# Turning the row maxima of a fused attention and expert block: one square of 128 columns for four tiles of 8, and one transfer for two

## The reference

```
def xattn(query, key, value):            # 16 heads of 16, B = 4, L = 512
    q = (query @ wq.T + bq)...; k = (key @ wk.T + bk)...; v = (value @ wv.T + bv)...
    scores = einsum('bhld,bhsd->bhls', q, k) / 4
    return einsum('bhls,bhsd->bhld', softmax(scores), v)

def ffn(src):                            # self attention with rotation, then experts
    q, k = rope(src @ Wq), rope(src @ Wk_c @ Wk); v = src @ Wv_c @ Wv
    sa = softmax(q k / 4) v @ Wo
    x = rmsnorm(src + sa, n1)
    shared = swiglu(x @ W_shared_in) @ W_shared_out
    routed = sum_e swiglu(x @ W1_shared) @ W2[e] * w[:, e]     # best 2 of 4 experts of the best group
    return rmsnorm(x + shared + routed, n2)

x = x + tanh(g_xattn) * xattn(layernorm(x), ctx, ctx)
x = x + tanh(g_ffn) * ffn(layernorm(x))
```

## Time and profile before

| what | value |
|---|---|
| median of 3 runs | 798.07 us (795.81 to 799.25) |
| profiled execution | 799.23 us, span 797.5 us |
| mean granted TensorE clock | 0.983 |
| busy: TensorE, weight loads | 752.8 us (94%), 347.6 us |
| busy: VectorE, ScalarE, GpSimd | 512.8, 417.4, 225.2 us |
| turned maxima L1607 | 128 matmuls, 217 to 221 ns, from 47.9 to 525.5 us |
| copy L782 | 32, 569 to 587 ns |
| transfers of the maxima L788 | 64 issues of 4 KB |

### The profile page before, as it was taken

The page is one execution under the profiler, slowest core; times in us unless marked ns, Lnnn a source line. Parts: engine busy times, 40 slices in busy tenths (PEclk is TensorE's granted clock), DMA queues, the critical chain, the costliest instruction groups (busy, mean ns, idle before and its releaser), DMA issues.

```text
span 797.5 us, 10572 instructions
## 1 busy us (share of the span) xinstructions
PE 752.8 (94%) x3606; PEld 347.6 (44%) x3606; DVE 512.8 (64%) x776; ACT 417.4 (52%) x766; POOL 225.2 (28%) x342
## 2 busy tenths in 40 slices
PE   5889999999999999999999999999999899989994
PEld 3432343343233233233423423426645755458883
DVE  2598848847868868878797798743366022523664
ACT  3447868877758767776675777683211122222000
POOL 3451123223315405304222410010105612400654
PEclk9989999999999999999999999999999999999998
DMA  8882233226124414413411331006003824000010
GB/s 244 222 240 62 59 106 121 80 51 200 47 57 164 108 41 136 129 41 94 144 42 41 125 105 52 1 2 210 1 0 134 274 100 132 0 0 1 34 40 34
DMA packets 51316, 73.32 MB, mean 92 GB/s; under 512 B 6976, under 2 KB 42304, under 8 KB 51264
## 3 DMA queue, kind: packets, MB, share of 16 engines
q1 hardware_dynamic: 47248, 63.80, 27.0%
q0 software_dynamic: 2816, 8.46, 2.8%
q10 hardware_dynamic: 1200, 0.40, 0.2%
HBM read 45.04 MB, written 27.33 MB: 91 GB/s over the span
## 4 chain that ended last, share of the span: by engine, by line
PE 75%; DVE 13%; ACT 6%; issue 3%; DMA 1%; POOL 1%; ACTq 1%; DVEq 0%; POOLq 0%
PE ps L1479 35%; PE ps L1627 11%; PE ps L1651 11%; PE ps L1599 10%; DVE negm L1135 7%; ACT hS L891 3%; PE ps L1474 2%; DVE bst L1013 2%; PE ps L1615 1%; PE ps L1607 1%; PE ps L1538 1%; DMA bv_bc<-in_L_xattn_bv_dram 1%; ACT rows L797 1%; PE ps L1533 1%; PE ps L1559 0%
## 5 line engine op out<-in xcount | busy, mean ns | idle before, releaser
L1135 DVE TENSOR_REDUCE negm<-ps 128x2 f32<-128x1024 f32 x256 | 304.9, 1223 | 80.4 <-PE ps L1599 73.3
L891 ACT ACTIVATE hS<-ps 128x512 f32<-128x512 f32 x512 | 278.5, 600 | 106.4 <-PE ps L1651 104.5
L1651 PE MATMUL ps<-w 98*128 98x512 bf16 x512 | 168.0, 386 | 5.9 <-ACT hS L891 3.3
L1599 PE MATMUL ps<-w 96*128 96x512 bf16 x512 | 154.6, 383 | 5.5 <-DVE negm L1135 4.9
L1627 PE MATMUL ps<-hS,mix 128*17 128x512 f32 x1024 | 134.7, 598 | 0.2
L1651 PEld LDWEIGHTS ps<-w 98*128 98x128 bf16 x512 | 42.5, 97 | 153.4 <-ACT hS L891 70.6
L1599 PEld LDWEIGHTS ps<-w 96*128 96x128 bf16 x512 | 49.0, 99 | 58.6 <-DVE negm L1135 11.5
L1331 DVE SCALAR_TENSOR_TENSOR ctxs<-qk,ps 128x512 f32<-128x512 f32 x32 | 22.0, 688 | 76.6 <-ACT qk L925 76.0
L925 ACT ACTIVATE qk<-ps 128x512 f32<-128x512 f32 x32 | 19.1, 597 | 82.5 <-PE ps L1479 78.6
L1479 PE MATMUL ps<-w,hS 128*128 x256 | 57.4, 387 | 2.0 <-issue 2.0
L1479 PEld LDWEIGHTS ps<-w,hS 128*128 128x128 f32 x256 | 49.7, 195 | 9.9 <-issue 2.8
(11 more groups left out here) (209 smaller groups left out, 891.6 us busy)
## 6 DMA issues: line engine op xcount, KB each, us to landing
w<-scrq SPq DMA_DIRECT2D x32, 384.0 KB, 4.1
scrk<-mix SPq DMA_DIRECT2D x24, 256.0 KB, 2.1
scrq<-mix SPq DMA_DIRECT2D x16, 384.0 KB, 3.3
scrq<-mix SPq DMA_DIRECT2D x24, 256.0 KB, 2.5
w<-scrk SPq DMA_DIRECT2D x32, 192.0 KB, 3.0
w<-scrk SPq DMA_DIRECT2D x32, 128.0 KB, 3.0
w<-in_L_ffn_W_experts_dram SPq DMA_DIRECT2D x8, 512.0 KB, 8.0
mix<-scrf SPq DMA_DIRECT2D x4, 528.0 KB, 5.6
```

The lines of the kernel that those rows point to most:

```text
L891: nc.scalar.activation(prob[:, kt % PROB_SLOTS, s % HG, :], slot_bank(("unit", u)), ACT.Exp, scale=SC).then_inc(s_exp, 1)
L1135: V.tensor_reduce(negm[:, gi % 2, 2 * t2:2 * t2 + 2, h], ps[:, bank:bank + 2, :], AX.X, ALU.max, negate=True).then_inc(s_re, 1)
L1599: last = MM(ps[:, bank + t, :], qs[0:STK, g, h, tt * P:(tt + 1) * P], ks[0:STK, g, h, :], start=True, stop=True)
L1651: MM(take(("unit", u)), ks[:, g, h, kt * P:(kt + 1) * P], qs[:, g, h, :], start=True, stop=True).then_inc(s_sT, 1)
```

## The change

The maxima are kept with heads outside and tiles inside, `m2` becomes a full square of 128 columns per parity of the group, of which 32 hold maxima (2 parts x 4 heads x 4 tiles) and 96 are zero, cleared once at the start. One transpose turns the square. ScalarE copies 32 partitions of 128 elements where it copied 8 of 512. One transfer takes all 32 partitions to the two stack rows; its semaphore is raised by 16 a group where the two raised it by 32.

```diff
+    MROWS = MPART * HG * TT
...
-        negm = sb("negm", [P, 2, TT, HG], F32)
-        m2 = sb("m2", [P, 2, TT, MPART, HG], BF16)
-        mTs = sb("mTs", [MPART * HG, 2, L], BF16)
+        negm = sb("negm", [P, 2, HG, TT], F32)
+        m2 = sb("m2", [P, 2, P], BF16)
+        mTs = sb("mTs", [MROWS, 2, P], BF16)
...
                 act.wait_ge(s_mtf, gi + 1)
-                ge(act, s_mrow, (gi - 1) * 16 * MPART)
-                nc.scalar.activation(mTs[:, gi % 2, :], slot_bank(("turned", gi))[:, 0:L // 2].bitcast(BF16)[0:MPART * HG, :],
+                ge(act, s_mrow, (gi - 1) * 16)
+                nc.scalar.activation(mTs[:, gi % 2, :], slot_bank(("turned", gi))[:, 0:P // 2].bitcast(BF16)[0:MROWS, :],
                                      ACT.Copy).then_inc(s_mts, 1)
...
-                for t in range(MPART):
-                    act.dma_start(qs[STK + t:STK + t + 1, gi % NG, :, :],
-                                  mTs[t * HG:(t + 1) * HG, gi % 2, :]).then_inc(s_mrow, 16)
+                act.dma_start(qs[STK:KROWS, gi % NG, :, :], mTs[:, gi % 2, :]).then_inc(s_mrow, 16)
...
+            V.memset(m2[:], 0.0).then_inc(s_ini, 1)
...
-                V.tensor_reduce(negm[:, gi % 2, 2 * t2:2 * t2 + 2, h], ps[:, bank:bank + 2, :], AX.X, ALU.max,
+                V.tensor_reduce(negm[:, gi % 2, h, 2 * t2:2 * t2 + 2], ps[:, bank:bank + 2, :], AX.X, ALU.max,
...
-                    m, o = negm[:, gi % 2], m2[:, gi % 2]
-                    link(V.tensor_copy(o[:, :, 0, :], m))
-                    mark(V.tensor_tensor(o[:, :, 1, :], m, o[:, :, 0, :], ALU.subtract))
+                    m = negm[:, gi % 2].rearrange("p h t -> p (h t)")
+                    o = m2[:, gi % 2, 0:MROWS].rearrange("p (s r) -> p s r", s=MPART)
+                    link(V.tensor_copy(o[:, 0], m))
+                    mark(V.tensor_tensor(o[:, 1], m, o[:, 0], ALU.subtract))
...
-                o = take(("turned", gi))[:, 0:L // 2].bitcast(BF16)
-                for tt in range(TT):
-                    last = TR(o[0:MPART * HG, tt * P:(tt + 1) * P],
-                              m2[:, gi % 2, tt].rearrange("p s h -> p (s h)"), identb[:])
+                o = take(("turned", gi))[:, 0:P // 2].bitcast(BF16)
+                last = TR(o, m2[:, gi % 2, :], identb[:])
                 last.then_inc(s_mtf, 1)
...
-                            pe.wait_ge(s_mrow, (gi + 1) * 16 * MPART)
+                            pe.wait_ge(s_mrow, (gi + 1) * 16)
```

More of the change, by code:

```diff
@@ L560, in _ @@
             load_x(3)
-            sp.wait_ge(s_mrow, 16 * MPART)
+            sp.wait_ge(s_mrow, 16)
             stack(1)
@@ L1005, in setup @@
                                       raw.rearrange("p (h j f) -> p f j h", f=2, j=DH // 2)[:, f]).then_inc(s_ini, 1)
-                dve.wait_ge(s_ini, 4 + EPG + 1 + 6)
+                dve.wait_ge(s_ini, 5 + EPG + 1 + 6)
                 dve.sem_inc(s_set, 1)
@@ L1138, in row_max @@
                     dve.wait_ge(s_re, c + 1)
-                    m, o = negm[:, gi % 2], m2[:, gi % 2]
-                    link(V.tensor_copy(o[:, :, 0, :], m))
-                    mark(V.tensor_tensor(o[:, :, 1, :], m, o[:, :, 0, :], ALU.subtract))
+                    if gi == 0:
+                        dve.wait_ge(s_ini, 5 + EPG)
+                    m = negm[:, gi % 2].rearrange("p h t -> p (h t)")
+                    o = m2[:, gi % 2, 0:MROWS].rearrange("p (s r) -> p s r", s=MPART)
+                    link(V.tensor_copy(o[:, 0], m))
+                    mark(V.tensor_tensor(o[:, 1], m, o[:, 0], ALU.subtract))
                     ready(s_m2)
@@ L1641, in _ @@
             pe.wait_ge(s_one, 2)
-            pe.wait_ge(s_ini, 4 + EPG)
+            pe.wait_ge(s_ini, 5 + EPG)
             for n in range(NI):
```

## The result

| what | before | changed |
|---|---|---|
| median of 6 runs each, same chip | 797.99 us (795.81 to 800.14) | 792.62 us (791.72 to 793.87) |
| profiled execution, span | 799.23, 797.5 us | 793.59, 791.8 us |
| from the turn for group 1 to that for group 31 | 464.74 us | 459.16 us |
| the same stretch in a second profile | 464.76 us | 459.12 us |

The ratio is 0.9933, with a 95% interval of 0.9914 to 0.9953. The forecast was 792.4.

A forecast was written before the change was run, and what follows sets the result against it. TensorE, busy 94% of the span, was taken as the bound. Gains of 2.03, 0.84, 0.91, 1.52 and 0.33 sum to 5.6 us, giving 792.4 against the median 798.07; forecast's own range 790.5 to 794.6, overall range 787 to 798.3.

The forecast's parts named there:

- the holes: TensorE gaps of 0.08 before and 0.09 after the four narrow turns; claimed to go with a square turn.
- full turns: Seven turns with no other engine near at the next maxima product: 0.29 gained each, 2.03 in all.
- last turn: After the final turn TensorE waits 0.33 for ScalarE; claimed gone, 0.33 gained.
- VectorE close: Seven turns where VectorE's L1154 ends shortly before the next maxima product: only 0.13 gained each, 0.91 in all.
- four ScalarE groups: Four groups where TensorE waits 0.38 for an exponential behind second issue and normalisation: wait gone whole, 1.52.
- The square at 0.11: Cost of one square turn on TensorE, read from float transposes L1615; maxima pair to score product 0.55 instead of 0.84.
- VectorE already last: Four turns where VectorE was taken to set the next maxima product: nothing gained from TensorE, only on ScalarE.
- The transfer: One issue of 32 pieces of 256 B; landing bounds 1.4 and 4.1, about 4.0 from issue to need, taken as hidden.
- the holes stay: Rival: the gaps are not the narrow tile's, a turn gains 0.17 instead of 0.29; 793.4, chance 0.08.
- VectorE takes it: Rival: VectorE's row maxima absorb TensorE's gain, leaving ScalarE's 1.85; 796.2, chance 0.16.
- More than I count: Rival: VectorE's limits move along with an earlier TensorE and each turn pays, 11.1 gained; 786.9, chance 0.12.
- Late landing: Rival: the small pieces arrive late and each group's first score product waits, 12.4 lost at 4.4; 804.9, chance 0.06.

The follow-up runs named there:

- run 1: Changed kernel with its one turn taking only the 32 columns that hold maxima: 792.5 us, ratio 0.9919 to the kernel before; stretch 459.74.
- run 2: Changed kernel with the square turned four times over instead of once: 790.37 us, ratio 0.9906 to the kernel before; stretch 459.39.
- run 10: Changed kernel with the turned square in the spare half of the heads' double bank, not a score-product bank: 793.27 us, ratio 0.9942; stretch 458.89.
- run 4: Kernel before with its two transfers joined into one of eight 1 KB pieces, narrow turns and long copy kept: 795.17 us, ratio 0.9969; stretch 463.18.
- run 6: Changed kernel with ScalarE's copy long again, each maximum written four times, 512 elements a partition: 791.15 us, ratio 0.9935; stretch 459.09.
- run 9: Changed kernel with the square cleared by GpSimd instead of VectorE, the wait kept: 792.26 us, ratio 0.9933; stretch 458.77.
- run 12: Kernel before plus one clearing of the whole maxima tile on VectorE and the wait for it: 800.12 us, ratio 1.0028; stretch 465.19.
- run 5: Changed kernel with the turn moved from step 9 to 11 and the transfer's issue from 11 to 12: 797.38 us, ratio 0.9997; stretch 463.50.
- run 3: Changed kernel with its transfer cut again into two issues, one per stack row: 793.26 us, ratio 0.9937; stretch 460.62.
- run 11: Changed kernel with the square both in the heads' spare half bank and cleared by GpSimd: 792.69 us, ratio 0.9941; stretch 458.59.

## Why the prediction was right, and where its terms were off

The time came out as forecast, 792.4 for 792.62, and so did the two mechanisms: the holes went with the narrow tile, and the wait in four groups went with the second issue. That the sums agree so closely, 5.63 for 5.68 over the turns, is luck. The term of the full turns came out 0.56 too large and that of the last turn 0.24; the term of VectorE close came out 0.53 too small and that of the four ScalarE groups 0.25.

- **The holes.** Right, and shown: 8 or 32 columns bring them, 128 columns don't. The Trainium skill, page TensorEngine Tiling (Array Packing), Key Properties, says that a change of tiling mode drains the array; runs 1 and 2 agree in so far as there are holes of 0.08 and 0.1 beside the narrow tile and none beside the full one. It does not say that a plain turn with few columns is such a change, and no run here tells a drain from another cause.
- **The square at 0.11** was too dear. The float transposes were the wrong row: this one is bf16 and steps by 0.06. TensorE's own part fell by 0.34, not 0.29.
- **The full gain of 0.29** was too large all the same: 0.21. The step that failed is "nothing is near". I looked at VectorE alone at the next maxima product. A second limit stood 0.14 behind: the slot that the turn takes, so that the second score product waits for the exponential (run 10). That is why runs 1 and 2, which give TensorE 0.19 and 0.165 more a turn, pay on average only 0.02 and 0.01 of it over the 30 turns of the stretch.
- **VectorE close, 0.13**, was too small: 0.21, as in the full turns. The limit of 0.15 behind L1154's end was read from 213.78 + 0.42 to 214.35. But that product comes 0.76 behind its turn, exactly as 390.75 to 391.51 in a turn where nothing is near. TensorE set it, not VectorE. In the changed kernel, where VectorE is last (214.34, the load waits for L1158), the distance is 214.29 to 214.35, 0.06. The two kinds were one, and the errors of their terms cancelled: the 14 turns gave 2.91, forecast 2.94. The same misreading stands in the four turns with "VectorE already last": before, TensorE set that product too. Nothing was gained there all the same, because the turn starts no earlier and VectorE is last now at the same 214.35.
- **The four turns of group 11's kind.** The wait went whole, but it was mis-sized: 0.54 each for 0.38. The term took the idle time in front of the product, and the price is the distance between the two products less their step, 0.76 - 0.22 (216.74, 217.50). The holes have no part in it. In group 23 most of it was given back. A maxima product there waits 0.40 for a row maximum on VectorE:

```profile
408.01 0.60 PE L1603 MATMUL ps<-w 96*128 96x512 bf16 x2 [0.40 <-DVE negm L1136]
```

 This is "what is late next", and I had named TensorE. Run 4 shows that the second issue was the cause of some four fifths of the gain in groups 11, 15 and 19 (about 0.45 of 0.54); run 6, that the copy's length had no part in it.
- **The last turn, 0.33**, failed: 0.09. The step that failed is "for the same reason". TensorE still waits 0.26 for the exponential, since what precedes it there is the exponentials themselves and not the second issue.

```profile
524.57 0.39 PE L1653 MATMUL ps<-w 98*128 98x512 bf16 x1 [0.26 <-ACT hS L891]
```

- **The clearing at nothing** was wrong by 0.35, through a stop of VectorE that no row of before could have told (runs 9 and 12).
- **The transfer** was hidden as forecast: 1.52 to land, with 4.1 or more from issue to need. But the forecast reads the landing off the last packet, and TensorE waits for the semaphore. In the changed kernel's trace its last count comes 1.9 to 2.0 behind the issue as a rule, 3.0 in group 22 and 3.6 in group 26, where the product comes 4.1 behind. In run 5, group 14, the last packet ends 2.3 behind the issue, the last count comes 3.3 behind, and the product that waits for it starts 3.36 behind. The Trainium skill, page DMA: Bandwidth & Descriptors, Why small descriptors are slow (HBM only), exempts transfers between on-chip tiles; here 32 pieces of 256 B end 1.51 behind their one issue and 8 of 1 KB (run 4) 1.45, 0.06 apart, which agrees.

Of the rivals, "the holes stay" fell with runs 1 and 2. "VectorE takes it" fell: its idle time for TensorE went only from 73.3 to 68.0, and one turn in 31 (group 23) lost most of its gain to a row maximum. "More than I count" was near on TensorE's side, 0.34 a turn, and was stopped by the slot. "Late landing" shows in two groups when the turn comes two steps later (run 5). By run 4, 1.56 of the gain is the single transfer's and 4.0 the turn's. Run 3 gives 1.46 for the transfer, but most of that is the two odd issues.

## What to carry to other kernels

Between wide products a small matmul can cost more than its step if its tile is narrower than the array (here 0.08 in front and 0.1 behind, with 8 and with 32 columns): fill the tile with zeros, which here cost nothing. The price of a wait is the distance between two starts less their usual step, not the idle time that the profile prints; and idle time of a weight load is no delay until its product is late. Before calling a distance a limit of the other engine, compare it with the same distance where that engine is early; if the two are equal, the engine in front sets it. Small gains in a pipeline with few shared banks are paid only up to the next slot's owner, so count that slot for each instruction moved, and measure on a stretch between two marks rather than on the total.

## What the runs showed of the hardware that was not expected

- A 128 x 128 bf16 turn in a stream of products steps by 0.055 to 0.06 us, the same as one of 8 columns; float ones step by 0.11.
- An issue of the maxima on ScalarE's queue lasts 0.51 to 0.73 as a rule, but three second issues of run 3 lasted 1.32, 1.22 and 1.66 (at 215.10, 290.62, 390.95). All that is queued behind waits: at 215.10 it was the normalisation, 1.05. Why these three were long is open.
- One clearing more on VectorE lengthened a stop between two of its instructions from 0.15 to 0.50, some 400 us later. The 0.50 stands in all nine profiles with the clearing on VectorE (the changed kernel twice, runs 1, 2, 3, 5, 6, 10 and 12), the 0.14 to 0.15 in all five without it (before twice, runs 4, 9 and 11).
